# A softmax's row maxima with the causal mask added by VectorE instead of by a product on TensorE

## The reference, cut to what matters

```python
xn = layernorm(x)                                     # x: (4, 1024, 256) fp32
Q, K, V = (xn @ w.T + b, split into 16 heads of 16)    # 64 (batch, head) pairs, T = 1024
S = einsum('hid,hjd->hij', K, Q) * 16 ** -0.5
delta = i - j
S = where(delta < 0, -inf, S) + where(delta < 0, 0, -delta)
C = softmax(S, axis=-1)
s = (C @ V, heads joined) @ o_w.T + o_b
g = silu(mixture of 8 experts, top 2 per token, on xn)
out = x + s * g
```

## Time and profile before

| | us |
|---|---|
| median of 3 runs | 803.21 (802.83 to 804.53) |
| profiled execution, its own time | 803.67 |
| its span in the trace | 801.9 |
| PE busy | 748.2 (93%) |
| DVE busy | 534.3 (67%) |
| ACT busy | 520.7 (65%) |
| POOL busy | 298.5 (37%) |

### The profile page before, as it was taken

One profiled execution on the slowest core, in us unless ns is written; L12 is line 12 of the kernel. 1 busy time (PEld: TensorE's weight loads), 2 busy tenths in 40 slices (PEclk: granted clock), 3 DMA queues, 4 the chain that ended last, 5 costly groups with the idle time before them and its releaser, 6 DMA issues.

```text
span 801.9 us, 16763 instructions
## 1 busy us (share of the span) xinstructions
PE 748.2 (93%) x5578; PEld 448.8 (56%) x5579; DVE 534.3 (67%) x1084; ACT 520.7 (65%) x1044; POOL 298.5 (37%) x342
## 2 busy tenths in 40 slices
PE   4999998999999999999999999999989999999894
PEld 2555553444544544554544544544438899999673
DVE  2456878788777777787787787787404544444287
ACT  3775556576666676676676676676786566666354
POOL 1342232252242553454343453434134457444300
PEclk9999999999999999999999999999999999999988
DMA  8789935254465575476475566495555755555496
GB/s 229 216 205 267 250 127 127 34 107 97 98 120 110 112 140 122 100 145 126 91 146 123 94 144 131 97 219 96 121 93 168 195 179 166 159 168 164 139 298 240
DMA packets 87302, 119.54 MB, mean 149 GB/s; under 512 B 16207, under 2 KB 60751, under 8 KB 87167
## 3 DMA queue, kind: packets, MB, share of 16 engines
q1 hardware_dynamic: 76686, 94.54, 51.0%
q0 software_dynamic: 10544, 24.07, 11.1%
HBM read 72.65 MB, written 45.55 MB: 147 GB/s over the span
## 4 chain that ended last, share of the span: by engine, by line
PE 69%; DVE 9%; DMA 8%; issue 7%; ACT 3%; POOL 2%; SPq 1%; ACTq 0%; POOLq 0%; DVEq 0%
PE ps L1394 16%; PE ps L1331 14%; PE ps L1380 13%; PE ps L1474 7%; PE ps L1496 7%; DVE mxa L981 6%; DMA arena<-y_dram 3%; PE ps L1383 3%; PE ps L1334 3%; DMA aug<-q_parts 2%; PE ps L1292 2%; PE ps L1457 2%; DMA q_parts<-arena 2%; POOL arena L646 2%; ACT arena L872 1%
## 5 line engine op out<-in xcount | busy, mean ns | idle before, releaser
L981 DVE TENSOR_REDUCE mxa<-ps 128x1 f32<-128x512 f32 (+3 forms) x608 | 363.0, 657 | 93.6 <-PE ps L1334 62.5
L872 ACT ACTIVATE arena<-ps 128x512 f32<-128x512 f32 x576 | 311.9, 604 | 148.8 <-PE ps L1383 128.6
L1331 PE MATMUL ps<-aug 105*128 105x512 bf16 (+3 forms) x768 | 228.8, 327 | 13.3 <-DVE mxa L981 9.2
L1380 PE MATMUL ps<-aug 108*128 108x512 bf16 (+3 forms) x768 | 216.2, 327 | 2.0 <-ACT arena L872 0.8
L1394 PE MATMUL ps<-arena,v_q 128*32 128x512 f32 (+3 forms) x1536 | 140.4, 491 | 3.7 <-ACT arena L872 3.7
L1331 PEld LDWEIGHTS ps<-aug 105*128 105x128 bf16 x768 | 74.8, 98 | 82.6 <-DVE mxa L981 34.2
L1380 PEld LDWEIGHTS ps<-aug 108*128 108x128 bf16 x768 | 66.1, 98 | 83.4 <-issue 32.5
L1383 PE MATMUL ps<-maskT_sb,idb 128*128 128x128 bf16 x512 | 112.4, 220 | 0.0
L1334 PE MATMUL ps<-mask_sb,idb 128*128 128x128 bf16 x512 | 98.6, 219 | 0.0
L778 POOL DMA_INDIRECT y_dram<-arena,y_row_of x71 | 68.6, 966 | 74.3 <-DVE arena L1231 72.8
L754 POOL DMA_INDIRECT xs_dram<-arena,slot x64 | 62.0, 969 | 76.8 <-ACT arena L872 38.1
(11 more groups left out here) (132 smaller groups left out, 715.9 us busy)
## 6 DMA issues: line engine op xcount, KB each, us to landing
aug<-k_parts SPq DMA_DIRECT2D x96, 128.0 KB
aug<-q_parts SPq DMA_DIRECT2D x96, 128.0 KB
arena<-xs_dram SPq DMA_DIRECT2D x71, 128.0 KB, 2.1
arena<-y_dram SPq DMA_DIRECT2D x16, 512.0 KB, 4.9
k_parts<-arena SPq DMA_DIRECT2D x16, 384.0 KB, 4.3
q_parts<-arena SPq DMA_DIRECT2D x16, 384.0 KB, 3.4
arena<-in_x SPq DMA_DIRECT2D x8, 512.0 KB, 5.9
xn_dram<-arena SPq DMA_DIRECT2D x8, 512.0 KB, 7.5
```

The source lines that it names most:

```text
L872: nc.scalar.activation(probs[SLOT[k, u]][:, half], score_bank(q, i), ACT.Exp).then_inc(exp_done, 1)
L981: nc.vector.tensor_reduce(mxa[:, h:h + heads, col_], src, AX.X, ALU.max).then_inc(piece_used, 1)
L1331: ins = nc.tensor.matmul(out_, k_aug[n][0:SCORE_ROWS, h0 + h, ib * P:(ib + 1) * P], q_aug[n][0:SCORE_ROWS, h0 + h, lo:lo + width], start=T ...
L1380: ins = nc.tensor.matmul(out_, q_aug[n][0:ALL_ROWS, h, jb * P:(jb + 1) * P], k_aug[n][0:ALL_ROWS, h, i0:i0 + hi - lo], start=True, stop=lo ...
```

## The change

The mask products of the first pass go. DVE adds the mask itself, in a `tensor_tensor_reduce` that writes `piece + mask` back to the bank and gives the row maximum of the sum. It takes one head at a time, so a piece on the diagonal becomes 4, 2 or 1 such operations. The added tensor is `wide_mask`: the mask in bf16, with enough zeros in front of it for the unmasked columns; for that the mask now lies right behind the zeros in one tensor, `blank`. Where the block has an off-diagonal piece, the operation starts its maximum from the column that the earlier `tensor_reduce` wrote (and DVE waits for itself until that column is there), so the merge in `split_maxima` goes too. Two waits for the zeros and the constants stand ahead of the first piece on DVE; the wait for the constants was behind the prologue before.

```diff
-        mask_sb = sb("mask_sb", [P, P], bf16)
...
-        zeros = sb("zeros", [P, D])
+        blank = sb("blank", [P, D + P // 2])
+        zeros = blank[:, 0:D]
+        wide_mask = blank[:, :].bitcast(bf16)
+        mask_sb = wide_mask[:, 2 * D:2 * D + P]
...
             def reduce_piece(s, banks, piece):
                 dve.wait_ge(piece_done, s + 1)
                 ib, lo, h, heads, width = PIECES[piece]
-                src = banks[:, 0:heads * width].rearrange("p (h j) -> p h j", h=heads)
-                col_ = ib if lo + width == P * (ib + 1) else TB // 2 + ib
-                nc.vector.tensor_reduce(mxa[:, h:h + heads, col_], src, AX.X, ALU.max).then_inc(piece_used, 1)
+                if lo + width < P * (ib + 1):
+                    nc.vector.tensor_reduce(mxa[:, h, TB // 2 + ib:TB // 2 + ib + 1], banks, AX.X, ALU.max).then_inc(piece_used, 1)
+                    return
+                if lo > 0:
+                    dve.wait_ge(piece_used, s - (HQ if heads == 1 else 1) + PIECE_BANKS + 1)
+                for n in range(heads):
+                    row = banks[:, n * width:(n + 1) * width]
+                    ins = nc.vector.tensor_tensor_reduce(
+                        out=row, in0=row, in1=wide_mask[:, 2 * D + P - width:2 * D + P], scale=1.0,
+                        scalar=mxa[:, h + n, TB // 2 + ib:TB // 2 + ib + 1] if lo > 0 else NEG,
+                        op0=ALU.add, op1=ALU.max, accum_out=mxa[:, h + n, ib:ib + 1])
+                ins.then_inc(piece_used, 1)
...
                 dve.wait_ge(piece_used, s + PIECE_BANKS + 1)
-                nc.vector.tensor_tensor(mxa[:, :, TB // 2:TB], mxa[:, :, TB // 2:TB], mxa[:, :, TB:],
-                                        ALU.max).then_inc(m_step, 1)
-                dve.wait_ge(m_step, 4 * q + 1)
                 nc.vector.tensor_copy(mparts[0], mxa[:, :, 0:TB]).then_inc(m_step, 1)
...
             ahead_of_windows = iter(list(enumerate(stream(0))))
+            dve.wait_ge(zeros_set, 1)
+            dve.wait_ge(consts_in, 16 * NCONST)
...
-            dve.wait_ge(consts_in, 16 * NCONST)
...
                 for h in range(heads):
                     out_ = banks[:, h * width:(h + 1) * width]
-                    diagonal = lo + width == P * (ib + 1)
                     ins = nc.tensor.matmul(out_, k_aug[n][0:SCORE_ROWS, h0 + h, ib * P:(ib + 1) * P],
-                                           q_aug[n][0:SCORE_ROWS, h0 + h, lo:lo + width], start=True, stop=not diagonal)
-                    if diagonal:
-                        ins = nc.tensor.matmul(out_[:, width - P:], idb[:, :], mask_sb[:, :], start=False, stop=True)
+                                           q_aug[n][0:SCORE_ROWS, h0 + h, lo:lo + width], start=True, stop=True)
```

More of the change, by code:

```diff
@@ L409, in many_zeros @@
         def many_zeros(n):
-            return bass.AP(zeros[:, :].tensor, zeros[:, :].offset,
-                           [list(zeros[:, :].ap[0]), [0, n], [1, D]])
+            return bass.AP(zeros.tensor, zeros.offset, [list(zeros.ap[0]), [0, n], [1, D]])
         best, first, second, gap, gexp, where, norm, low = col
@@ L433, in _ @@
                      "wv": (wvg_sb[:, :, 0:D], weights(wvT)), "gate": (wvg_sb[:, :, D:D + E], weights(gate)),
-                     "idb": (idb[:, :], ident_b), "mask": (mask_sb[:, :], mask_neg),
+                     "idb": (idb[:, :], ident_b), "mask": (mask_sb, mask_neg),
                      "maskT": (maskT_sb[:, :], mask_negT), "before": (before_sb[:, :], before),
@@ L636, in _ @@
             pool.sem_inc(split_done, 8)
-            nc.gpsimd.memset(zeros[:, :], 0.0).then_inc(zeros_set, 1)
+            nc.gpsimd.memset(zeros, 0.0).then_inc(zeros_set, 1)
             for n in range(AUG):
@@ L723, in clear_pads @@
                     nc.gpsimd.indirect_dma_start(
-                        out=xs_dram, in_=zeros[:, :], in_offset=None,
+                        out=xs_dram, in_=zeros, in_offset=None,
                         out_offset=bass.IndirectOffsetOnAxis(ap=pad_slot[:, e:e + 1], axis=0)).then_inc(xs_zero, 16)
@@ L978, in reduce_piece @@
                 ib, lo, h, heads, width = PIECES[piece]
-                src = banks[:, 0:heads * width].rearrange("p (h j) -> p h j", h=heads)
-                col_ = ib if lo + width == P * (ib + 1) else TB // 2 + ib
-                nc.vector.tensor_reduce(mxa[:, h:h + heads, col_], src, AX.X, ALU.max).then_inc(piece_used, 1)
+                if lo + width < P * (ib + 1):
[10 more added lines that the diff above has]
+                ins.then_inc(piece_used, 1)
             def split_maxima(q, s):
                 dve.wait_ge(piece_used, s + PIECE_BANKS + 1)
-                nc.vector.tensor_tensor(mxa[:, :, TB // 2:TB], mxa[:, :, TB // 2:TB], mxa[:, :, TB:],
-                                        ALU.max).then_inc(m_step, 1)
-                dve.wait_ge(m_step, 4 * q + 1)
                 nc.vector.tensor_copy(mparts[0], mxa[:, :, 0:TB]).then_inc(m_step, 1)
-                dve.wait_ge(m_step, 4 * q + 2)
+                dve.wait_ge(m_step, 3 * q + 1)
                 nc.vector.tensor_tensor(mrest[:, :, :], mxa[:, :, 0:TB], mparts[0], ALU.subtract).then_inc(m_step, 1)
-                dve.wait_ge(m_step, 4 * q + 3)
+                dve.wait_ge(m_step, 3 * q + 2)
                 nc.vector.tensor_copy(mparts[1], mrest[:, :, :]).then_inc(m_step, 1)
-                dve.wait_ge(m_step, 4 * q + 4)
+                dve.wait_ge(m_step, 3 * q + 3)
                 nc.vector.tensor_tensor(mparts[2], mrest[:, :, :], mparts[1], ALU.subtract).then_inc(m_split, 1)
```

## The result

| | before | after |
|---|---|---|
| median, first measurement (4 and 4 runs) | 803.87 us | 834.86 us |
| ratio, 95% interval | | 1.0352 (1.0308 to 1.0397) |
| profiled execution, its own time | 803.67 | 835.17 |
| its span | 801.9 | 833.2 |
| mean granted clock of that execution | 0.992 | 0.982 |

The change makes the kernel slower, by 31 us in the measurement that the prediction is about. The chips differ: the unchanged kernel took 804, 824, 835 and 841 us in four measurements.

The account below looks back on a forecast made before the run. DVE's own steps plus its starving during PE's batches were taken to set a quad's time: +5.0 - 1.6 - 0.9 - 0.2 = +2.3 us, x 14 = +32, prologue +2, giving 837 us; range 802 to 880.

Parts of the forecast that it names:

- The sums: DVE, first-pass diagonal pieces: 32 sums with maxima per quad, eight each of 512, 384, 256 and 128 columns, 13.1 us.
- The readout: DVE, second instruction of each pair, reading out one column: 0.10 us each, 32 per quad, 3.2 us.
- The column operand: DVE: 16 sums per quad start from a column of mxa instead of a constant, 0.06 us each, 1.0 us.
- The self-waits: DVE waits for its own last piece in three places per quad (blocks 4 and 5): 0.3 us.
- What the starving gives back: DVE's stops during PE's value batches shrink per quad: 1.6 us from longer-lasting backlog, 0.9 from the first and short stops.
- The mask products: PE loses 32 products per quad, 1.9 us; nearly all becomes waiting, 0.2 us a quad is gained.
- cheap pair: Rival: readout 0.077 us and the full 1.2 us of starving recovered; +1.6 a quad, 822 us; lower part of main case.
- How many quads: Of 15 intervals between splits, 14 count, since the first ends beside projections: 14 x 2.3 = +32 us.
- The prologue: 67 to 126 us: about 7 us more DVE work against 12 idle, PE loses 2.9; +2, ends -3 and +7.
- The tail: Behind 569 us: DVE has 2.5 us of work in 33, so nothing changes.
- the drained readout: Rival: DVE's readout waits for the sum, 0.18 + 0.08 us instead of 0.10; +5.8 a quad, about 891 us; chance 0.12.
- Faster: Rival: readout costs nothing and column operand overlaps, so PE's lost products decide; -0.8 a quad, about 792 us; chance 0.12.

Follow-up runs that it names:

- e7: Kernel before plus 32 short reduces (40 columns) a quad on VectorE into a tensor nothing reads; 853.75 us, ratio 1.028 on chip C.
- e3: Changed kernel with every maximum started from a constant, no self-waits, the merge back; ratio 1.017 on chip A, 1.019 (850.29 us) on C.
- e5: Changed kernel with each pair replaced by a plain sum, no maximum or readout, so the output differs; 821.52 us, ratio 0.998 on chip B.
- e1: Kernel before without the first pass's 32 mask products per quad, VectorE's instructions unchanged, scale and decay altered; 822.90 us, ratio 0.977 on chip A.
- e2: Changed kernel with mask products back on PE, VectorE adding zeros; ratio 1.014 on chip A; run again on C, 850.48 us, 1.023.
- e4: Kernel before with pairs, and no mask product, only in the 16 one-head diagonal pieces; merge kept; 841.08 us, ratio 1.000 on chip A.
- e6: Kernel before with only the reduces of diagonal pieces split by head, 32 instead of 22 a quad; 825.34 us, ratio 1.001 on chip B.
- after_beside: The changed kernel, unchanged, run beside the kernel before on chip C; 851.55 us, ratio 1.025.
- before_again: The kernel before, unchanged, run again for its trace on chip B; 824.40 us, ratio 1.000.

## Why the prediction was right, and where it was not

837 us was said and 834.9 measured. The direction and the mechanism were right; that the number came so near is luck, since two terms were off in opposite directions: the quads cost 24 us where 32 were said, and falls of the clock, which no step had, brought 8. The range, 802 to 880, was wide enough to take in no change at all, so the quad's account below says more than the hit.

- **What bounds the quad.** Right in the main, and now tested: DVE's time sets most of it although PE showed 99% (e7, and e3 and e5 the other way), and PE's lost products come out as waiting. But PE counts beside it more than I had it. With DVE's instructions unchanged its mask products cost 0.8 us a quad (e1), and the 0.49 taken as DVE's step at 384 columns was PE's pace.
- **The sums.** 13.1 us predicted. Plain sums step by 0.60 at 512 and 0.465 at 384 columns (e5: 4 x 0.60 + 3 x 0.465 = 3.80); with steps of 0.33 and 0.20 at 256 and 128, that is 8 x 1.60 = 12.8. Right, though 1.02 ns a column from 0.60 would have given 0.47 at 384 columns, where the 0.49 of the reduces was put.
- **The readout.** 0.10 us each, 3.2 a quad. Measured 0.044 to 0.05 each over a plain sum, 1.4 to 1.6 a quad, and that holds the maximum too. This is the step that was mis-sized most. I stayed above the row of 0.077 where I should have asked whether the next instruction can start before the readout ends; the trace shows that it starts with it. By the rule of the Trainium skill that I had cited ("Vector Engine (DVE) Microarchitecture Reference", section 5.2, about 75 ns for each instruction) it would be 2.4 us. The measured step is below that too.
- **The column operand.** 0.06 predicted from the durations of another operation, 0.027 measured (754 against 727 ns): 0.4 us a quad instead of 1.0.
- **The self-waits.** 0.3 predicted, 0.7 measured: from 322.57 with two reduces behind each other (0.60 each) the chained sum should follow at 323.77 and starts at 324.00; the three places cost 0.2 to 0.3 each. e3 gives them and the column operands, less the merge that it puts back, as 0.83 us of interval.
- **Together** DVE's steps are 9.6 + 12.8 + 1.6 + 0.4 + 0.7 + 1.1 = 26.2 us where 28.3 was said: +2.9, not +5.0. (The parts of the 23.3 add up to 23.2, which changes nothing.)
- **What the starving gives back.** 2.5 us predicted, 1.25 measured: the large stops are now 1.46, 1.15, 1.10 and 1.03 us, 4.74 together against 5.99. The short one is gone as I said, but the others hardly shrank. The prediction let three mean pieces of 0.71 us wait in the banks at each batch. But what DVE works off ahead of these stops is mostly plain reduces, whose step stays at 0.60:

```profile
329.63 2.48 DVE L981 TENSOR_REDUCE mxa<-ps 128x1 f32<-128x512 f32 x4
333.20 0.62 DVE L987 CUSTOM_DVE_ANT_0 ps<-ps,blank,mxa 128x384 f32<-128x384 f32 x1 [1.10 <-PE ps L1338]
...
335.36 2.48 DVE L981 TENSOR_REDUCE mxa<-ps 128x1 f32<-128x512 f32 x4
337.75 0.75 DVE L987 CUSTOM_DVE_ANT_0 ps<-ps,blank,mxa 128x512 f32<-128x512 f32 x1
...
339.59 0.76 DVE L987 CUSTOM_DVE_ANT_0 ps<-ps,blank,mxa 128x512 f32<-128x512 f32 x1 [1.03 <-PE ps L1338]
```

Four reduces stand ahead of the stop of 1.10, four and one pair ahead of that of 1.03, two ahead of that of 1.15.

- **The mask products.** 0.2 predicted; 0.3 with pairs (e2), 0.8 without (e1).
- **The quad:** +2.9 - 1.25 = +1.65 by these terms, +1.6 measured, +2.3 predicted. The mechanism was that of the "cheap pair" case (+1.6).
- **How many quads.** 14 were counted. All 15 intervals are longer, the first by 1.0: 15 x 1.6 = 24 us.
- **What was missing: the clock.** Five intervals of the changed kernel show a clock of 0.95 between 149 and 602 us, of which three stand above, and the kernel before had 1.00 there in that measurement. 33.00 and 32.9 against 31.35 make 1.6 us each, 8 us in all. 24 + 8 is near the 32.7 found between the splits. No step of the prediction had this. How much of the 8 the change causes is not shown: in the traces of chip B the kernel before has two falls there and the changed one five, and the mean clocks over the runs are 0.985 and 0.982.
- **The prologue** +2, measured 0.0. **The tail** 0, measured -1.4, in which I see no cause.

Of the rivals, the drained readout is excluded by the step of 0.65 us. "Faster" needed a readout under 0.04 with a free column operand. The measured 0.044 to 0.05 is close to that point, but the operand is not free, and the self-waits, there at 0.3, cost 0.7. e4, with 16 pairs and neither of these two, is level. The signs named beforehand: pairs of 0.65 and 0.25 us (said 0.70 and 0.31), intervals of 31.3 to 33.0 (said 31 to 33) but for three of 34.0, 35.9 and 38.2, DVE at 82% (344 of 419 us; said 85 to 90), PE's waits 7.0 us a quad on the rows above, against 1.5 and a few short ones.

No version beat the kernel before with the whole computation done: e4 and e6 are level with it, and e1's gain is that of a kernel that leaves the mask out.

## What to carry to other kernels

An engine that is 99% busy need not be the bound: look for the stops of the engine that feeds on it, and test with work that only takes time (e7). Test the busy engine as well, by taking work off it alone (e1): here both counted. To price a stop, look at which instructions are queued ahead of it, not at the mean one. When two small maxima are fused by chaining, count the self-wait: three times 0.24 us cost more than the merge of 0.2 us that they replaced. And relieving TensorE in a kernel that waits elsewhere can buy nothing at all: here 32 products a quad less brought 0.3 us in the quad, a clock of 0.976 instead of 0.987, and the same time (e2_again against after_beside). Take the mean clock and the times of several runs into the comparison, not only the interval of one quad.

## What the runs showed of the hardware that I had not expected

**The granted clock falls to 0.50 in the middle of this kernel, where PE is busy most of the time.** In the quad that starts at 404.50, its first 3 us, then the 3.4 us that follow the fall:

```profile
404.50:407.50 3.00, 1.37 (x10) 0.69 (x9) 2.86 (x17) 1.59 (x4) 1.62 (x2) 1.00 0.15 47
```

```profile
407.90:411.30 3.40, 3.40 (x27) 0.96 (x20) 0.73 (x5) 0.00 (x0) 0.00 (x0) 0.50 0.06 7
```

A batch of value products that runs in this stretch takes 3.36 us, at the level of 1.2 GHz; the same batch two quads earlier, at 2.4 GHz, took 1.93:

```profile
407.58 3.36 PE L1399 MATMUL ps<-arena,v_q 128*32 128x256 f32 x24
```

```profile
344.86 1.93 PE L1399 MATMUL ps<-arena,v_q 128*32 128x256 f32 x24
```

Ahead of the fall PE was busy 1.37 of 3.00 us, and what ended its waits there was DVE, at work on the split and the eight short pairs behind it; in the kernel before the first 3 us of a quad have 2.89:

```profile
299.57:302.57 3.00, 2.89 (x34) 1.88 (x35) 2.83 (x9) 2.22 (x5) 1.20 (x2) 1.00 0.13 44
```

Four of the five falls of the changed kernel start 2.5 to 3.9 us behind a split. But a pause like this does not always bring a fall: the quad of 341.79 has 1.38 us in its first 3 and none. On C the kernels with all of the first pass's mask products on PE have higher mean clocks than those without, 0.984 to 0.987 against 0.976 and 0.974, whatever their speed. On B it is 0.985 and 0.988 against 0.982 and 0.981, a small difference. On A it is 0.982 and 0.986 against 0.981 and 0.972, where before and e1 (0.982 and 0.981) can't be told apart. That the products themselves hold the clock up is shown by one pair only (e2_again against after_beside, 0.987 and 0.976, every run of the one above every run of the other), and it gave the same time. Why e3, with shorter pauses (1.80 us busy in the first 3 of its quad), has the lowest clock is open.

**A readout that is recorded with 140 ns costs at most 44 to 50 ns**, the maximum included, since the next operation starts with it. **The same program took 804, 824, 835 and 841 us in four measurements**, three of them on three different chips. In the one trace of it from a slower measurement (before_again) single intervals are 0.6 to 7.4 us longer, with falls of the clock, a late DMA, or a stop that no wait in the profile explains.
